# Where the low halves of queries and keys are computed in the attentions with maxima

## The reference, cut to what matters

```python
Q = (hs @ q_w + q_b).reshape(B, S, H, HD).transpose(0, 2, 1, 3)
K = (hs @ k_w + k_b).reshape(B, S, H, KPH).transpose(0, 2, 1, 3)
V = (hs @ v_w + v_b).reshape(B, S, H, KPH).transpose(0, 2, 1, 3)
scores = jnp.einsum('bhsk,bhtk->bhst', Q[..., :KPH], K) / math.sqrt(KPH)
attn = jax.nn.softmax(scores, axis=-1)
ao = jnp.einsum('bhst,bhtv->bhsv', attn, V)
```

## Time and profile before

| | us |
|---|---|
| three timed runs | 1726.0, 1734.0, 1737.9 (median 1734.0) |
| profiled execution, its own time | 1747.2 |
| profiled execution, span from first to last instruction | 1745.5 |
| VectorE busy in the span | 1272.4 |
| ScalarE busy in the span | 1068.0 |
| GpSimd busy in the span | 693.3 |
| mean granted clock of TensorE, share of full speed | 0.935 |

### The profile page before, as it was taken

One profiled execution on the slowest core, in us unless ns is written; L12 is line 12 of the kernel. 1 busy time (PEld: TensorE's weight loads), 2 busy tenths in 40 slices (PEclk: granted clock), 3 DMA queues, 4 the chain that ended last, 5 costly groups with the idle time before them and its releaser, 6 DMA issues.

```text
span 1745.5 us, 34465 instructions
## 1 busy us (share of the span) xinstructions
PE 1524.6 (87%) x12731; PEld 1091.4 (63%) x12741; DVE 1272.4 (73%) x2817; ACT 1068.0 (61%) x2219; POOL 693.3 (40%) x801
## 2 busy tenths in 40 slices
PE   6588778799998898899899999998889999989975
PEld 5344446578877555668678767665548984755542
DVE  2688862697775898479999677758854448758988
ACT  4499942367765676389999155547754443147765
POOL 3456536578887022356767313230000111511223
PEclk9799989899999999988988999999989998799985
DMA  3200121200000000010000100000000000000000
GB/s 133 111 13 14 42 87 39 59 10 2 1 1 1 2 2 2 4 37 1 2 1 1 58 2 2 2 13 2 1 2 1 1 1 11 0 19 2 2 1 25
DMA packets 14791, 30.94 MB, mean 18 GB/s; under 512 B 1537, under 2 KB 10145, under 8 KB 13857
## 3 DMA queue, kind: packets, MB, share of 16 engines
q1 hardware_dynamic: 13602, 26.63, 4.4%
q0 software_dynamic: 1024, 2.10, 0.4%
HBM read 22.42 MB, written 6.29 MB: 16 GB/s over the span
## 4 chain that ended last, share of the span: by engine, by line
PE 48%; ACT 14%; DVE 13%; POOL 13%; issue 11%; DMA 1%; another core or an unknown queue 0%; SPq 0%; POOLq 0%; DVEq 0%; ACTq 0%
PE PS L1420 5%; PE PS L1473 4%; ACT big L2262 4%; POOL big L837 4%; PE PS L1745 3%; DVE negmax L2803 3%; PE PS L1734 3%; POOL big L825 3%; ACT big L2240 2%; POOL big L833 2%; PE PS L1912 2%; PE PS L1495 2%; PE PS L1896 2%; PE PS L1325 2%; PE PS L1399 2%
## 5 line engine op out<-in xcount | busy, mean ns | idle before, releaser
L2240 ACT ACTIVATE big<-PS 128x1024 f32<-128x1024 f32 (+1 forms) x256 | 249.4, 975 | 160.3 <-PE PS L1427 159.8
L2803 DVE TENSOR_REDUCE negmax<-PS 128x4 f32<-128x1024 f32 x192 | 234.7, 1223 | 59.6 <-PE PS L1420 54.7
L1420 PE MATMUL PS<-KS,QS 32*128 32x256 f32 (+1 forms) x1152 | 134.4, 318 | 33.9 <-DVE negmax L2803 20.4
L1420 PEld LDWEIGHTS PS<-KS,QS 32*128 32x128 f32 x1152 | 88.0, 188 | 108.0 <-ACT big L2240 75.8
L711 POOL TENSOR_TENSOR rstd<-veps,mhalf 128x2 f32<-128x2 f32 x72 | 51.4, 714 | 241.3 <-DVE veps L2677 231.8
L1427 PE MATMUL PS<-QS,KS 32*128 32x256 f32 (+1 forms) x1152 | 134.7, 321 | 1.4 <-ACT big L2240 1.4
L1473 PE MATMUL PS<-big,V 128*32 128x256 f32 (+1 forms) x2048 | 134.9, 382 | 0.0
L737 POOL TENSOR_TENSOR res<-resb,XB 128x256 f32<-128x256 f32 x24 | 17.5, 728 | 254.7 <-ACT resb L2326 254.7
L779 POOL TENSOR_SCALAR KT<-QT 128x1024 f32<-128x1024 f32 x64 | 66.7, 1042 | 64.8 <-DVE QT L2822 62.9
L2822 DVE SCALAR_TENSOR_TENSOR QT<-PS,wint 128x1024 f32<-128x1024 f32 x64 | 77.3, 1219 | 16.1 <-PE PS L1365 15.5
L1427 PEld LDWEIGHTS PS<-QS,KS 32*128 32x128 f32 x1152 | 85.4, 188 | 5.5 <-issue 3.7
(11 more groups left out here) (479 smaller groups left out, 4331.5 us busy)
## 6 DMA issues: line engine op xcount, KB each, us to landing
W<-in_wpack SPq DMA_DIRECT2D x1, 4180.0 KB, 14.0
W<-in_wpack SPq DMA_DIRECT2D x1, 2560.0 KB, 8.9
W<-in_wpack SPq DMA_DIRECT2D x1, 2449.5 KB, 8.1
y_rows<-one_more SPq DMA_DIRECT2D x1, 2048.0 KB, 10.4
masks<-in_mask SPq DMA_DIRECT2D x8, 256.0 KB, 2.8
x_rows<-x_tok SPq DMA_DIRECT2D x16, 128.0 KB, 2.1
W<-in_wpack SPq DMA_DIRECT2D x1, 1538.0 KB, 6.1
x_tok<-in_x SPq DMA_DIRECT2D x1, 1024.0 KB, 5.0
```

What stands on the lines that cost most here:

```text
L1420: mm = nc.tensor.matmul(PS[:, MAXB[half], o], QS[r, bm % 2, tm, j * P:(j + 1) * P], KS[r, bm % 2, tm, k], start=not a.causal, stop=last)
L2240: nc.scalar.activation(PX[:, T % 2, 2 * p:2 * p + 2, 0:cols], PS[:, exp_banks(g)[0]:exp_banks(g)[0] + 2, 0:cols], ACT.Exp, scale=a.scale). ...
L2803: ins = nc.vector.tensor_reduce(negmax[:, h:h + 2, :].rearrange("p h j -> p (h j)"), banks.rearrange("p h (j k) -> p (h j) k", j=2), AX.X, ...
```

## The change: what it does

In `L1x`, `L2f` and `L3x` ScalarE, behind each high part, also writes the same projection with its bias, not rounded, to SBUF (`unsplit`: tiles 4 to 7 of `KT`, two pairs in turn), and only then signals `t_hi`. GpSimd subtracts the high part from it (`low_part`, now for all these stages). VectorE's `low` stays for `L0x` alone. On GpSimd the low parts of batch i+1 come first in the loop's turn i; batch 0's come behind `clear_v` in `L1x` and `L3x`. For `L2f`, batch 0's stand in the last turn of `L2x`'s loop, ahead of its last residual sum, and those of batches 1 to 7 stand at the beginning of GpSimd's `L2f` program, ahead of the bias split and `twice`.

```diff
+        def unsplit(b, k):
+            return KT[:, 4 + 2 * (b % 2) + k, :]
@@ GpSimd @@
+            def low_part(a, b):
+                for k in range(2):
+                    pool.wait_ge(sem("t_hi"), before(a.name, "t_hi") + 2 * b + k + 1)
+                    nc.gpsimd.tensor_tensor(HL[:, k, 1, :], KT[:, 2 * (b % 2) + k, :] if a.rope else unsplit(b, k),
+                                            HL[:, k, 0, :].bitcast(F32), ALU.subtract).then_inc(sem("t_lo"), 1)
...
-                def low_part(b):
-                    for k in range(2):
-                        pool.wait_ge(sem("t_hi"), at("t_hi", 2 * b + k + 1))
-                        nc.gpsimd.tensor_tensor(HL[:, k, 1, :], KT[:, 2 * (b % 2) + k, :], HL[:, k, 0, :].bitcast(F32),
-                                                ALU.subtract).then_inc(sem("t_lo"), 1)
...
                 for i in range(-2, B + 2):
-                    if a.rope and 0 <= i + 1 < B:
-                        low_part(i + 1)
+                    if 0 <= i + 1 < B and (n != "L2f" or i >= 0):
+                        low_part(a, i + 1)
+                    if n == "L2x" and i == B + 1:
+                        low_part(ATTNS["L2f"], 0)
...
             def L2f():
                 pool.wait_ge(*loaded("L2f"))
+                for b in range(1, B):
+                    low_part(ATTNS["L2f"], b)
@@ ScalarE, high(b) @@
                             ins = nc.scalar.activation(HL[:, k, 0, :], PS[:, XB_BANK, k * S:(k + 1) * S], ACT.Identity,
                                                        bias=w(f"{n}_b{x}"))
+                            if not a.clip:
+                                if b >= 2:
+                                    act.wait_ge(sem("t_lo"), at("t_lo", 2 * (b - 1)))
+                                ins = nc.scalar.activation(unsplit(b, k), PS[:, XB_BANK, k * S:(k + 1) * S], ACT.Identity,
+                                                           bias=w(f"{n}_b{x}"))
                         ins.then_inc(sem("t_hi"), 1)
@@ VectorE @@
-                    if not a.rope and (b := due(g, a.project_at + 1)) is not None:
+                    if a.clip and (b := due(g, a.project_at + 1)) is not None:
                         low(b)
```

## The result

The changed kernel took 1770.9 us (median of 4 runs, 1769.1 to 1776.2) against 1734.0 before: 1.0217 times as long, 95% interval 1.0187 to 1.0248, so 36.9 us slower. Forecast were 1751.9 and 1736 to 1769. The direction is right, the size is twice the forecast. The profiled execution took 1769.6 (span 1767.9).

The account below looks back on a forecast made before the run. The prediction took a ring as the bound: scores, maximum and exponential side by side, next scores. Copies 11.9, starts 3.0 and clock 3.0 gave +17.9 us on the median 1734.0: 1751.9, range 1736 to 1769.

Parts of the forecast that it names:

- VectorE loses the low parts: Three stages' low parts leave VectorE: 22.9 us of busy time, but only 0.05 to 0.06 us a batch gained.
- Maxima at a flat 0.54: Sign that the forecast is right: VectorE's maxima always start 0.54 us behind their scores.
- ScalarE's copies: Two more activations ahead of step 8b-6's exponential delay the next scores; batches 2 to 7 of three stages, together 11.9 us.
- GpSimd at nothing in steady batches: GpSimd's subtractions in steady batches finish 0.7 us or more before TensorE asks for them, so they cost nothing.
- a wait of the spread matmul: Where TensorE reads the low parts: if GpSimd's cover went, one extra 0.7 us a batch would show here.
- Starts: First low parts of each stage come later: +1.9 in `L1x`, +0.6 in `L2f`, +0.45 in `L3x`, together 3.0 us.
- The stretched subtraction: GpSimd's subtractions at stage starts might be slowed by VectorE's SBUF work; upper bound 5 us for the starts.
- The clock: TensorE idles more in `L1x` and `L2f`, so two more falls to 1.2 GHz at 1.5 us each: +3.
- The ring: Steady steps: scores, then maximum and exponential side by side, then next scores; it sets the pace and carries 11.9 us.
- VectorE is the bound: Rival: VectorE sets the pace in 24 batches, so removing low parts gives -18.7 us, 1715.3; chance 0.07.
- the copies are hidden: Rival: ScalarE's idle time absorbs its added activations, only stage starts cost, 1736.1 us; chance 0.13.
- The clock falls in every batch: Rival: added idling lowers TensorE's clock in all 18 steady batches, +14.9 and +22.5, 1771.4 us; chance 0.20, full or half.

Follow-up runs that it names:

- before again: The kernel before, unchanged, run and profiled a second time: 1734.4 us, ratio 1.0003; its profiled execution took 1732.9.
- the one at 1733.7: The kernel before with 8 matmuls of constants (1.7 us) added ahead of `L3a`: 1741.8 us, ratio 1.0046; its profiled execution took 1733.7.

## Why the forecast was right in direction and short in size

- *VectorE loses the low parts, worth 0.05 to 0.06 a batch*: right. Maxima at a flat 0.54; with the low parts gone the maximum of step 8b-5 comes 0.05 sooner, and the time is 0.9992.
- *ScalarE's copies, +0.68, +0.68 and +0.62 in 18 batches*: right. 1.50, 2.60, and 16.59 against 15.90 in `L1x`, 0.69; 16.17 against 15.53 in `L2f`, 0.64; 16.76 against 16.07 in `L3x`, 0.69. Four activations of a batch start 0.36 apart. The copies alone make the kernel as slow as the whole change.
- *GpSimd at nothing in steady batches*: right, with more than a microsecond of cover (627.44 to 628.58). With the copies behind the exponential the pair ends 3.67 behind the scores of step 8b-6 and not 2.43. The cover is gone, and it shows as a wait of the spread matmul, 0.18 in `L1x` and 0.48 in `L2f`, as the prediction had said.
- *Starts, 3.0*: 2.95. The stretched subtraction isn't there: the pair in `L2f` took 1.45 beside VectorE's memset. The Trainium skill, "GPSIMD Engine Reference", section "1. Specifications", makes two SBUF inputs of VectorE, or a mode of it that uses two ports, the condition of contention. A memset has no input; whether it uses both ports no run shows, and the 1.45 shows no contention.
- *The clock, +3, "two more falls"*: this is the step that failed. The ring's and the starts' 14.9 stand, so clock and the rest are 36.9 - 14.9 = 22. Three things were wrong in it.
  First the size inside the changed stages. Against before again they grew by 8.0 + 7.7 + 6.2 = 21.9 us, of which the ring explains 11.9; 10 is the clock. Against the profile that I worked from it is 7. The count of falls was not far off: that profile has five in these stages (in `L2f` four, of which I missed the first, from 1180 on, and one in `L3x`), the kernel after has eight (three in `L1x`, three in `L2f`, two in `L3x`). But I priced each at 1.5 us, as the short one that I had looked at. They last 3 to 10 us here; the one from 1236 on makes a batch 19.14 and not 16.17. By the granted clock the three stages spent some 51 us at 1.2 GHz, against 24 in the profile that I worked from and 17 in before again.
  Then the place. I looked for the clock only where the idling was added. Against before again the piece behind `L2f` grew by 10.8 and that ahead of it by 5.2, of which 0.5 and 0.6 are starts, while the piece up to `L1x` was 1.3 shorter. Most of the 10.8 is one stretch in `L3a`, and that was in the profile from which I worked.
  Last the base. I noted that this profile lay 13 us above the median and said that only differences carry over. But they carry over only if the base has the same falls. Measured between the two profiled executions, the change cost 1769.6 - 1747.2 = 22.4, near the forecast's 17.9: both have the stretch. The forecast of 1751.9 set that difference upon a median 13 us lower. That most runs of before lack the stretch is my guess from the profile at 1732.9; the one at 1733.7 that has it warns against it.
- What ties the clock in the changed stages to the change is all profiles together. In the seven with the ring of before (the low parts left out or not) the granted clock is 1.00 in `L1x`, 0.92 to 1.00 in `L2f` and 0.99 in `L3x`. In the five with the copies ahead of the exponential and the wait unfilled it is 0.94 to 0.95, 0.81 to 0.90 and 0.95 to 0.96. No range overlaps.
- The rivals: *VectorE is the bound* and *the copies are hidden* fell with the runs above. *The clock falls in every batch* gave 1771.4, almost the measured number, but not by its mechanism: three of the six steady batches of `L1x` run at full clock (one is shown below) and eleven of the twelve in `L2f` and `L3x`, and about half of the excess lies in stages that it doesn't speak of.

The windows of the kernel after: a low stretch inside `L1x`, a whole steady batch at 1.00 (16.59 us, against 15.90), and the stretch in `L3a`.

```profile
594.00:601.00 7.00, 7.00 (x74) 3.83 (x70) 4.50 (x8) 5.32 (x8) 0.00 (x0) 0.55 0.01 2
...
627.61:644.20 16.59, 14.57 (x176) 9.09 (x176) 13.86 (x29) 12.91 (x22) 5.22 (x7) 1.00 0.00 1
```

```profile
1523.50:1543.50 20.00, 20.00 (x68) 15.69 (x68) 12.84 (x28) 3.30 (x8) 10.35 (x11) 0.50 0.00 0
```

What stays open: why the stretch in `L3a` comes in one execution and not in another, which no run shows, and how much of the clock's share in the changed stages is owed to the waits and how much to where the stages lie. The split of the 22 us is that of single profiles: another pair would divide it otherwise. No version here beats the kernel before; the run without low parts bounds what could be won at some 6 us (0.9965), so I looked for none.

## What to carry to other kernels

Follow the ring from scores to scores and not the busy shares: here VectorE, busy 92% of a steady stretch, was rid of 22.9 us of instructions for nothing, and 0.73 us ahead of an exponential on a half-idle engine went into every batch. Putting the new work behind the ring's instruction helps only if whoever reads its result, and whatever else waits in that engine's queue, has the time; here neither had, and it gave back about 1 of 12 us. And where TensorE's clock moves, compare pieces of several profiles, the untouched ones too, with the granted clock beside each; a difference read from a single profile that lies above the median of the timed runs can't be set upon that median for a forecast of a per cent.

## What the runs showed of the hardware that I had not expected

A long stretch at 1.2 GHz needs no idling in it, nor just ahead of it. In `L3a` TensorE is busy 20.00 of 20.00 us and stays at 0.50. The output loop there has turns of four spread and eight output matmuls; the timeline of TensorE in the kernel after, then the same work in the kernel before again:

```profile
1531.45 2.08 PE L2020 MATMUL PS<-W,V 128*128 128x128 f32 x8
1533.45 0.79 PE L2011 MATMUL PS<-QS,HL 32*128 32x512 f32 x1
...
1535.45 2.08 PE L2020 MATMUL PS<-W,V 128*128 128x128 f32 x8
```

```profile
1498.47 1.16 PE L2013 MATMUL PS<-W,V 128*128 128x128 f32 x8
1499.56 0.50 PE L2004 MATMUL PS<-QS,HL 32*128 32x512 f32 x1
...
1500.69 1.16 PE L2013 MATMUL PS<-W,big 128*128 128x128 f32 x8
```

A turn takes 4.00 us against 2.22. Ahead of the stretch TensorE had run at 1.00 in this stage, for the larger part in this loop, busy 21.73 of 22.00:

```profile
1500.00:1522.00 22.00, 21.73 (x128) 15.58 (x126) 17.32 (x21) 2.10 (x2) 14.27 (x9) 1.00 0.00 1
```

So the busy time, then or just before, doesn't tell that the clock will fall. (Ends of matmuls are modelled, so this is the profile's busy time and no more.) The Trainium skill, "TensorE: Matmul & The Clock Gate", section "What's actually happening", says that the clock follows how busy the array has been. By that, read as the profile's busy time, this stretch would not be there; the measurement decides, and busy time here is no guide to it. The same section says that the chip's observation doesn't restart with a kernel, so that the point at which the clock rises depends on when the first matmul comes. It says this of a kernel's start; a stretch in `L3a` that comes and goes with the same instructions is in line with it, and no run here shows that this is the reason.
